# Token products of a router and LoRA kernel: three matmuls of 200 columns against one of 400 and one of 200

## The reference

```python
base = x @ W.T                                     # (2048, 1024)
logits = x @ Wr.T + one_hot(language) * 5.0        # (2048, 8)
gates = two largest logits, softmax over them      # (2048, 8), zero elsewhere
y = base + 2.0 * sum_e gates_e * (x @ A_e.T) @ B_e.T
hits = softmax(y @ centroids.T / 0.1) > 0.01       # (2048, 64)
query_sel, cluster_sel = hits.any(1), hits.any(0)
dense = y @ V.T + bias
out = x + where(query_sel & cluster_sel[assignments], dense, 0)
```

## Time and profile before

| | us |
|---|---|
| median of 3 runs | 349.85 |
| profiled execution | 350.19 |
| its span | 348.1 |
| first matmul of the first token product | 62.57 |
| transposes that end the second stage | 165.71 |

### The profile page before, as it was taken

How to read it: one execution, slowest core, us unless ns; L and a number is a source line. 1 busy time by engine, 2 the same in 40 slices (tenths; PEclk the granted TensorE clock), 3 DMA queues, 4 the chain that set the end, 5 groups by cost and what they waited for, 6 DMA issues and landing times.

```text
span 348.1 us, 4828 instructions
## 1 busy us (share of the span) xinstructions
PE 337.4 (97%) x1892; PEld 296.7 (85%) x1892; DVE 254.1 (73%) x439; ACT 134.0 (39%) x215; POOL 1.0 (0%) x9
## 2 busy tenths in 40 slices
PE   6799999999999999999999999999999999999993
PEld 6588888999999999999887888888888888888882
DVE  2627669557787787788976979849498494984926
ACT  4616464334564555645452422333223332233120
POOL 1000000000000000000000000000000000000000
PEclk9999999999999999999999999999999999999997
DMA  7576440345334333333813162733707336060303
GB/s 270 188 274 265 154 183 16 105 124 180 118 100 148 122 121 122 124 119 122 316 47 122 60 225 79 247 115 123 240 1 247 117 124 237 2 241 0 122 0 121
DMA packets 13782, 49.10 MB, mean 141 GB/s; under 512 B 1664, under 2 KB 1664, under 8 KB 13760
## 3 DMA queue, kind: packets, MB, share of 16 engines
q1 hardware_dynamic: 13760, 48.80, 40.1%
HBM read 40.41 MB, written 8.39 MB: 140 GB/s over the span
## 4 chain that ended last, share of the span: by engine, by line
PE 94%; DMA 2%; DVE 2%; issue 1%; ACT 0%; SPq 0%; DVEq 0%
PE ps L925 31%; PE ps L926 31%; PE ps L927 31%; DMA vt_raw<-in_v 2%; PE ps L985 1%; DVE u L838 0%; DVE vt_lo L580 0%; ACT vt_hi L393 0%; DVE u L902 0%; DVE u L814 0%; DVE nat L908 0%; DVE u L583 0%; ACT u L393 0%; PE ps L1047 0%; SPq L307 0%
## 5 line engine op out<-in xcount | busy, mean ns | idle before, releaser
L925 PE MATMUL ps<-vt_hi,w_hi 128*128 128x288 f32 (+1 forms) x216 | 71.4, 330 | 3.1 <-DVE vt_lo L580 3.1
L926 PE MATMUL ps<-vt_lo,w_hi 128*128 128x288 f32 (+1 forms) x216 | 70.4, 326 | 0.0
L927 PE MATMUL ps<-vt_hi,w_lo 128*128 128x288 f32 (+1 forms) x216 | 70.4, 326 | 0.0
L393 ACT ACTIVATE u<-ps 128x512 f32<-128x512 f32 x32 | 19.1, 598 | 88.5 <-PE ps L927 59.0
L926 PE MATMUL ps<-gop_lo,sl_s_hi 128*128 128x512 f32 x128 | 49.8, 389 | 0.0
L925 PEld LDWEIGHTS ps<-vt_hi,w_hi 128*128 128x128 f32 x216 | 40.6, 188 | 6.6 <-DVE vt_lo L580 2.4
L926 PEld LDWEIGHTS ps<-vt_lo,w_hi 128*128 128x128 f32 x216 | 40.6, 188 | 2.8
L927 PEld LDWEIGHTS ps<-vt_hi,w_lo 128*128 128x128 f32 x216 | 40.5, 188 | 2.8
L925 PE MATMUL ps<-gop_hi_t,sl_s_hi 128*128 128x512 f32 x96 | 37.5, 390 | 0.0
L927 PE MATMUL ps<-gop_hi_t,sl_s_lo 128*128 128x512 f32 x96 | 37.4, 389 | 0.0
L925 PE MATMUL ps<-aw_hi,xt_hi 128*128 128x200 f32 x128 | 35.5, 278 | 0.1
(11 more groups left out here) (123 smaller groups left out, 637.3 us busy)
## 6 DMA issues: line engine op xcount, KB each, us to landing
xt_raw<-in_xt SPq DMA_DIRECT2D x32, 512.0 KB, 4.0
nat<-in_x SPq DMA_DIRECT2D x16, 512.0 KB, 4.3
out<-nat SPq DMA_DIRECT2D x15, 512.0 KB, 2.7
wraw<-in_w SPq DMA_DIRECT2D x9, 512.0 KB, 3.4
w_raw<-in_w SPq DMA_DIRECT2D x8, 512.0 KB, 3.3
vt_raw<-in_v SPq DMA_DIRECT2D x4, 576.0 KB, 4.5
vt_raw<-in_v SPq DMA_DIRECT2D x4, 512.0 KB, 7.3
awt_raw<-in_awt SPq DMA_DIRECT2D x1, 544.0 KB, 6.0
```

Source lines behind the costliest of these rows:

```text
L393: return nc.scalar.activation(dst, src, ACT.Copy)
L925: nc.tensor.matmul(dst, l_hi, r_hi, start=start, stop=False, skip_group_check=True)
L926: nc.tensor.matmul(dst, l_hi, r_lo, start=False, stop=False, skip_group_check=True)
L927: return nc.tensor.matmul(dst, l_lo, r_hi, start=False, stop=stop, skip_group_check=True)
```

## The change

The 400 columns of `aw` now lie side by side: hi of A and Wr (136), hi of the centroids' part (64), its rest (64), and the rest of A and Wr (136). A k-step is then two matmuls: the rounded x against all 400 columns, and the rest of x against the first 200. The columns' sums with the rests stand apart in PSUM and are added afterwards: ACT copies those of A and Wr (272 values for the pair) to `aw_rest`, DVE adds them to the router logits and to h; ACT copies those of the cluster logits (128 values for the pair) to `hits`, DVE adds them there, and maximum and exp read `hits`. The correction `lora_logits` is done in the same manner with `gb`: 128 columns and 64. `ROUTER_STEPS` goes from 11 to 13 and `SOFT_STEPS` from 7 to 8. `take_rest(n-1)`, ACT's copy to `aw_rest`, stands between the rounded copy of x for c = 0 and `r_part` or `t_part`.

```diff
+LO_A = AWG + C
+LO_END = LO_A + AW
...
-            aw_hi = sb("aw_hi", [P, KD, AWG], F32R, sweeps)
-            aw_lo = sb("aw_lo", [P, KD, AWG], F32R, sweeps)
+            aw = sb("aw", [P, KD, LO_END], F32R, sweeps)
...
+            aw_rest = sb("aw_rest", [P, 2, AW], F32, sweeps)
...
+            def take_rest(n):
+                for c in range(2):
+                    act.wait_ge(aw_ready[c], n + 1)
+                if n >= 1:
+                    act.wait_ge(router, ROUTER_STEPS * (n - 1) + 6)
+                copy(aw_rest[:], ps_aw(n)[:, :, LO_A:LO_END]).then_inc(rest_taken, 1)
...
             def softmax_exp(n):
-                act.wait_ge(soft, SOFT_STEPS * n + 2)
+                act.wait_ge(logits_ready, n + 1)
                 if n >= 1:
-                    act.wait_ge(soft, SOFT_STEPS * (n - 1) + 5)
+                    act.wait_ge(soft, SOFT_STEPS * n)
+                copy(hits[:], ps_aw(n)[:, :, AWG:LO_A]).then_inc(logits_rest, 1)
+                act.wait_ge(soft, SOFT_STEPS * n + 3)
                 for c in range(2):
-                    nc.scalar.activation(ex[:, c, :], ps_aw(n)[:, c, AW:AWG], ACT.Exp, bias=negb[:, c:c + 1],
+                    nc.scalar.activation(ex[:, c, :], hits[:, c, :], ACT.Exp, bias=negb[:, c:c + 1],
...
             for n in range(NPAIR):
                 if n >= 1:
                     split_x(0, n)
+                    take_rest(n - 1)
...
             def route(n):
...
-                for c in range(2):
-                    dve.wait_ge(aw_ready[c], n + 1)
-                nc.vector.tensor_tensor(rl[:], aw[:, :, ER:AW], lang_bias[:, n:n + 1, :].broadcast_to([P, 2, E]),
+                dve.wait_ge(rest_taken, n + 1)
+                nc.vector.tensor_tensor(rl[:], sums[:, :, ER:AW], aw_rest[:, :, ER:AW], ALU.add).then_inc(router, 1)
+                dve.wait_ge(router, base + 1)
+                nc.vector.tensor_tensor(rl[:], rl[:], lang_bias[:, n:n + 1, :].broadcast_to([P, 2, E]),
                                         ALU.add).then_inc(router, 1)
...
                 nc.vector.tensor_tensor(diff[:].unsqueeze(2), m8[:, :, 1:2], m8[:, :, 0:1],
                                         ALU.subtract).then_inc(router, 1)
+                nc.vector.tensor_tensor(hg[:], sums[:, :, 0:ER], aw_rest[:, :, 0:ER], ALU.add).then_inc(router, 1)
...
             def softmax_max(n):
...
-                dve.wait_ge(logits_ready, n + 1)
-                nc.vector.tensor_reduce(mx[:], ps_aw(n)[:, :, AW:AWG], AX_X, ALU.max).then_inc(soft, 1)
+                dve.wait_ge(logits_rest, n + 1)
+                nc.vector.tensor_tensor(hits[:], ps_aw(n)[:, :, AW:AWG], hits[:], ALU.add).then_inc(soft, 1)
                 dve.wait_ge(soft, base + 1)
+                nc.vector.tensor_reduce(mx[:], hits[:], AX_X, ALU.max).then_inc(soft, 1)
...
             def token_product(c, n):
...
-                    last = three(ps_aw(n)[:, c, 0:AWG], xt_hi[c][:, k, :], xt_lo[c][:, k, :], aw_hi[:, k, :],
-                                 aw_lo[:, k, :], k == 0, k == KD - 1)
+                    nc.tensor.matmul(ps_aw(n)[:, c, 0:LO_END], xt_hi[c][:, k, :], aw[:, k, :], start=(k == 0),
+                                     stop=(k == KD - 1), skip_group_check=True)
+                    last = nc.tensor.matmul(ps_aw(n)[:, c, 0:AWG], xt_lo[c][:, k, :], aw[:, k, 0:AWG], start=False,
+                                            stop=(k == KD - 1), skip_group_check=True)
...
             def lora_logits(n):
...
-                    last = three(ps_aw(n)[:, c, AW:AWG], hgt_hi[:, t], hgt_lo[:, t], gb_hi[:], gb_lo[:], False, True)
+                    nc.tensor.matmul(ps_aw(n)[:, c, AW:LO_A], hgt_hi[:, t], gb[:], start=False, stop=True,
+                                     skip_group_check=True)
+                    last = nc.tensor.matmul(ps_aw(n)[:, c, AW:AWG], hgt_lo[:, t], gb[:, 0:C], start=False, stop=True,
+                                            skip_group_check=True)
```

More of the change, by code:

```diff
@@ L42 @@
 S1, S2, S3, S4 = range(4)
-ROUTER_STEPS = 11
-SOFT_STEPS = 7
+ROUTER_STEPS = 13
+SOFT_STEPS = 8
 WARM_UP = 24
@@ L76, in adaln_ffn_kernel @@
         ident = sb("ident", [P, P], F32)
-        gb_hi = sb("gb_hi", [P, C], F32R)
-        gb_lo = sb("gb_lo", [P, C], F32R)
+        gb = sb("gb", [P, 2 * C], F32R)
         onehot_a = sb("onehot_a", [C, FO], BF16)
@@ L210, in adaln_ffn_kernel @@
         router = sem("router")
+        rest_taken = sem("rest_taken")
+        logits_rest = sem("logits_rest")
         e2_ready = sem("e2_ready")
@@ L448, in _ @@
                 copy(gb3_raw[:, 0:2, 0:A1] if m == 0 else raw_of(m - 1, slice(0, A1)), halves)
-                copy(gb_hi[:] if m == 0 else aw_hi[:, m - 1, AW:AWG], src[:, 2 * A1:HALF]).then_inc(g_evicted, 1)
+                copy(gb[:, 0:C] if m == 0 else aw[:, m - 1, AW:AWG], src[:, 2 * A1:HALF]).then_inc(g_evicted, 1)
                 if 2 <= m < 2 + PIECES:
@@ L453, in _ @@
                     act.wait_ge(awt_landed, 16)
-                    copy(aw_hi[:, :, 0:AW], awt_raw[:]).then_inc(awt_hi, 1)
+                    copy(aw[:, :, 0:AW], awt_raw[:]).then_inc(awt_hi, 1)
                 if m == KD:
@@ L464, in evict @@
                      halves).then_inc(g_evicted, 1)
+            def take_rest(n):
[4 more added lines that the diff above has]
+                copy(aw_rest[:], ps_aw(n)[:, :, LO_A:LO_END]).then_inc(rest_taken, 1)
             def router_exp(n):
-                act.wait_ge(router, ROUTER_STEPS * n + 4)
+                act.wait_ge(router, ROUTER_STEPS * n + 5)
                 nc.scalar.activation(e2[:], diff[:], ACT.Exp).then_inc(e2_ready, 1)
@@ L542, in _ @@
             r_part(KH - 1, slice(A1, HALF), chunk_number(KD - 1, 1))
+            take_rest(NPAIR - 1)
             t_part(KH - 1)
@@ L661, in _ @@
                 if m == 0:
-                    rest(gb_lo[:], cent, gb_hi[:]).then_inc(cent_split, 1)
+                    rest(gb[:, C:2 * C], cent, gb[:, 0:C]).then_inc(cent_split, 1)
                 else:
-                    rest(aw_lo[:, m - 1, AW:AWG], cent, aw_hi[:, m - 1, AW:AWG]).then_inc(cent_split, 1)
+                    rest(aw[:, m - 1, AWG:LO_A], cent, aw[:, m - 1, AW:AWG]).then_inc(cent_split, 1)
                 if 2 <= m < 2 + PIECES:
@@ L668, in _ @@
                     dve.wait_ge(awt_hi, 1)
-                    rest(aw_lo[:, :, 0:AW], awt_raw[:], aw_hi[:, :, 0:AW]).then_inc(awt_split, 1)
+                    rest(aw[:, :, LO_A:LO_END], awt_raw[:], aw[:, :, 0:AW]).then_inc(awt_split, 1)
                 if m == 7:
@@ L679, in route @@
                 base = ROUTER_STEPS * n
-                aw = ps_aw(n)
-                for c in range(2):
-                    dve.wait_ge(aw_ready[c], n + 1)
-                nc.vector.tensor_tensor(rl[:], aw[:, :, ER:AW], lang_bias[:, n:n + 1, :].broadcast_to([P, 2, E]),
+                sums = ps_aw(n)
+                dve.wait_ge(rest_taken, n + 1)
+                nc.vector.tensor_tensor(rl[:], sums[:, :, ER:AW], aw_rest[:, :, ER:AW], ALU.add).then_inc(router, 1)
+                dve.wait_ge(router, base + 1)
+                nc.vector.tensor_tensor(rl[:], rl[:], lang_bias[:, n:n + 1, :].broadcast_to([P, 2, E]),
                                         ALU.add).then_inc(router, 1)
-                dve.wait_ge(router, base + 1)
+                dve.wait_ge(router, base + 2)
                 for c in range(2):
                     nc.vector.max(m8[:, c, :], rl[:, c, :]).then_inc(router, 1)
-                dve.wait_ge(router, base + 3)
+                dve.wait_ge(router, base + 4)
                 nc.vector.tensor_tensor(diff[:].unsqueeze(2), m8[:, :, 1:2], m8[:, :, 0:1],
                                         ALU.subtract).then_inc(router, 1)
+                nc.vector.tensor_tensor(hg[:], sums[:, :, 0:ER], aw_rest[:, :, 0:ER], ALU.add).then_inc(router, 1)
                 for c in range(2):
                     nc.vector.max_index(idx8[:, c, :], m8[:, c, :], rl[:, c, :]).then_inc(router, 1)
-                dve.wait_ge(router, base + 6)
+                dve.wait_ge(router, base + 8)
                 nc.vector.tensor_tensor(pick[:], iota8[:].unsqueeze(1).unsqueeze(1).broadcast_to([P, 2, 2, E]),
@@ L698, in route @@
                 nc.vector.tensor_scalar(den[:], e2[:], 1.0, 1.0 / SCALING, ALU.add, ALU.mult).then_inc(router, 1)
-                dve.wait_ge(router, base + 8)
+                dve.wait_ge(router, base + 10)
                 nc.vector.reciprocal(wts[:, :, 0], den[:]).then_inc(router, 1)
-                dve.wait_ge(router, base + 9)
+                dve.wait_ge(router, base + 11)
                 nc.vector.tensor_tensor(wts[:, :, 1], wts[:, :, 0], e2[:], ALU.mult).then_inc(router, 1)
-                dve.wait_ge(router, base + 10)
+                dve.wait_ge(router, base + 12)
                 nc.vector.tensor_tensor(pick[:], pick[:], wts[:].unsqueeze(3).broadcast_to([P, 2, 2, E]),
                                         ALU.mult).then_inc(router, 1)
```

(14 more changed lines are left out.)

## The result

The changed kernel takes 346.05 us (median of 5 runs, 344.67 to 347.32), the kernel before 349.69 in the same set: ratio 0.9893, 95% interval 0.9861 to 0.9925. It is faster by 3.6 us, forecast 4.3. What the change did has to be read between the start of the first token product and that of the third stage.

What follows compares the result with a forecast made beforehand. PE's matmul queue was taken to bound the kernel: 7.2 us saved there, less waits for DVE of 1.4 in even rounds and 1.5 at the second stage's end, is -4.3, from 349.85 to 345.5 us; range 343.5 to 348.2.

Steps and rivals of the forecast that it cites:

- What bounds: Whole kernel: one queue of matmuls on PE, busy 337.4 of 348.1 us, waiting for nobody after the start.
- PE's sum: Second stage: token products save 0.34 us each, 5.4 in all, logits' corrections 1.8; together 7.2 us off PE's queue.
- The load as a floor: PE matmuls below about 240 columns: the weight load, running beside one matmul, sets the step at 0.111 us.
- the rival: Narrow-matmul run's token products: width sets the step and loads run ahead, so pairs 0.236 us apart; no chance given.
- The even rounds: Second stage, n = 2, 4, 6: PE waits 0.46 us for the hgt split, 1.4 in all; rounds of 12.15.
- my row of additions: DVE per pair: start 0.32 us later, then delays of 0.31, 0.21 and 0.34; exps reading SBUF taken as costing nothing.
- The end of the stage: Transposes before the third stage: no cover for hg, so PE waits 1.5 us, the largest single item given back.
- Sum: Whole kernel: -7.2 saved on PE, +1.4 and +1.5 of waits, together -4.3 us.
- Rival 2's second leg: PE's weight loads: a load runs ahead, 2.1 us off PE, DVE returns over half: 344.9; whole rival's chance 0.18.
- its first: DVE and ACT additions: cover holds; at half cost 343.5 us, with nothing added and no wait 342.6; whole rival's chance 0.18.
- Rival 3: Token products: 400 columns cost 0.22 to 0.227 us, so only corrections save, 1.8; about 349.3, no change; chance 0.08.
- Rival 4's mechanism: DVE chain from correction to transposes becomes the bound; at twice the prices PE waits every round, +3.8 us, 353.7; chance 0.09.

Runs made afterwards that it cites:

- the control just told: Kernel before, with three of four t_sums subtractions on GpSimd and route(7) first at the end of the second stage: second stage 103.28 us, one time 351.87.
- the narrow one: Changed kernel with the second matmul of each pair (rest of x) 64 columns wide instead of 200: pairs 0.295 us apart, odd rounds 11.68.
- the changed kernel's second execution: Changed kernel run again beside its variants, no edit: 345.11 us against 349.58 for the kernel before, ratio 0.9873.

## Why the prediction was right

- **What bounds.** PE's queue, with no wait in the second stage: borne out by the control just told, where lighter DVE work changed nothing.
- **PE's sum.** Forecast for the stage: 16 x 0.34 + 7 x 0.22 = 7.0. Measured: the stage shrank by 3.76 and holds 3.14 of waits, so 6.9. A token product saves 0.33, not 0.34 (rounds of 12.36 with three matmuls of 200, of 11.70 without additions); a correction saves 0.22. Two small errors in the token product's term partly cancelled: the pair takes 0.294 and not 0.291, but the triple that it replaces repeats at 0.335 and not 0.333.
- **The load as a floor.** Right, against a rule: by the Trainium skill ("TensorE: Matmul & The Clock Gate", Architectural detail) PE's queue pulls weight loads ahead. If this had run the load behind a short matmul ahead of it, 64 and 200 columns would have given different pairs. They give 0.295 and 0.294, where the rival asked 0.236 of the narrow one.
- **The even rounds.** Forecast a wait of 0.46 and rounds of 12.15; measured 12.23 against 11.70, a wait of 0.53. DVE was 0.06 later than my row of additions said, in the two exps, whose reading of SBUF I had put at nothing: 0.31 before, and in ACT's timeline of the changed kernel

```profile
103.84 0.35 ACT L497 ACTIVATE ex<-hits,negb 128x64 f32<-128x64 f32 x1 [0.88 <-DVE negb L743]
...
104.18 0.33 ACT L497 ACTIVATE ex<-hits,negb 128x64 f32<-128x64 f32 x1
```

  DVE's steps on either side of the exps start 1.01 apart here, 0.94 before (106.74 to 107.68):

```profile
103.63 0.17 DVE L743 TENSOR_SCALAR negb<-mx 128x2 f32<-128x2 f32 x1
104.64 0.17 DVE L748 RECIPROCAL rsum<-esum 128x2 f32<-128x2 f32 x1 [0.84 <-ACT ex L497]
```

- **The end of the stage.** Forecast 1.5, measured 1.55: the two chunks take 7.87 to the transposes' start where they took 6.38, and the transposes 0.05 more. Additions alone give 1.21 there (1.2 by the same reckoning).
- **Sum.** Forecast -4.3; in the two profiled executions -3.76 - 0.27 = -4.03, that is 7.17 saved and 3.14 of waits, against 7.2 and 2.9: the miss of 0.27 is in the waits but for 0.03. The medians gave -3.6 and -4.5; that the first set's median of 346.05 lies so near the forecast 345.5 is in part luck, since the first stage moves single times by more.
- **Rivals.** Rival 2's second leg (a load that runs ahead) fell with the narrow matmul; its first is true only if the additions or as much other work leave DVE. Rival 3 fell: the wide matmul costs 0.183. Rival 4's mechanism is real but its price was not reached: DVE binds in three rounds of seven and at the end of the stage. The variant with the 400-column matmul alone shows the state that it described.

## What to carry to other kernels

When an engine is always busy, ask how late every other queue may become before it holds it up: here 2.4 us in a round for hg, about 1.4 for the split of the turned hg in an even round, and nothing at the end of the stage. The last two ran out; together they gave back 3.1 of the 7.2 us saved, half of it at the end of the stage. Below the width at which a matmul takes as long as the load of the next weights (an estimated 240 columns here, on the line through 288 and 512), columns are free. Joining narrow products that share their stationary operand saves a whole load's step of 0.11 us while the joined one stays under that width, as in the correction, and less above it: 0.04 for 400 columns. What is joined has to be added elsewhere. Work moved to an idle engine pays only if it does not slow the engine that it relieves, so place it beside that engine's slack and not beside its critical steps.

## What was not expected

GpSimd's subtractions lengthened two DVE groups beside them by 60% (0.42 to 0.67) and 107% (0.28 to 0.58), though neither waited for the other's semaphore. The other DVE operations in the same time kept their length: the logits' add, which reads PSUM, 0.29, and the row sums between the two, 0.28. What sets the two apart was not tried.

The first stage varies by nearly as much as the change is worth. PE does the same work there in all these kernels, and in their profiled executions the first token product starts anywhere between 61.16 and 64.39 us. The stretch from 8 to 34 us of the variant without additions (64.39):

```profile
8.00:34.00 26.00, 25.07 (x98) 20.04 (x99) 12.38 (x16) 11.22 (x17) 0.00 (x0) 0.87 0.60 219
```

and of the changed kernel's second execution (61.16):

```profile
8.00:34.00 26.00, 25.66 (x112) 20.89 (x113) 15.00 (x20) 13.02 (x19) 0.00 (x0) 1.00 0.67 255
```

The granted clock is 0.87 instead of 1.00 there, a mean of both levels: 0.61, 0.50, 0.50 and 0.69 in the four stretches of 2 us from 8 on (0.50 is 1.2 GHz), then 1.00. Fewer bytes moved; PE had waited 2.9 us for the first splits of V, and 1.7 in the other. Of the 13 profiled executions four show the lower level near the start, and their first token product starts at 62.73, 64.29, 64.29 and 64.39; in the nine others the clock stays at 1.00 and it starts between 61.16 and 62.57. Whether the late loads let the clock fall was not tried, and idle time of PE alone does not foretell it: from 10 to 12 us PE is busy for 1.12 us in the variant without additions, with the clock at 0.50, and for 0.59 us in the kernel before, with the clock at 1.00.

```profile
10.00:12.00 2.00, 1.12 (x3) 0.50 (x2) 1.72 (x2) 1.55 (x3) 0.00 (x0) 0.50 0.91 358
```

```profile
10.00:12.00 2.00, 0.59 (x3) 0.50 (x4) 1.83 (x2) 1.58 (x3) 0.00 (x0) 1.00 0.92 340
```
 For a small change the length of the stage in question, which repeated to 0.06 us, says more than the whole.
